# Attention over edges: a node block's sums kept and rescaled in four PSUM banks, and copied out at every step by ScalarE or VectorE

## The reference, cut to what matters

```python
q = (x @ Wq + bq).reshape(n, H, C)          # H = 8 heads, C = 32
k = (x @ Wk + bk).reshape(n, H, C)
v = (x @ Wv + bv).reshape(n, H, C)
alpha = einsum('ehc,ehc->eh', q[dst], k[src]) / sqrt(C)
amax = segment_max(alpha, dst)
ex = exp(alpha - amax[dst])
denom = segment_sum(ex, dst)
msg = (v[src] * (ex / denom[dst])[:, :, None]).reshape(-1, H * C)
out = segment_sum(msg, dst) + x @ Ws + bs
```

## Time and profile before

| | |
|---|---|
| median of the runs | 3828.62 us (3827.41, 3828.62, 3846.94) |
| the profiled execution, device time | 3797.8 us |
| its span | 3796.1 us |
| granted PE clock, mean over the span | 0.788 |
| DVE busy over the span | 2055.0 us (54%) |
| ACT busy over the span | 1393.1 us (37%) |
| PE busy over the span | 2511.5 us (66%) |

### The profile page before, as it was taken

The page is one execution under the profiler, slowest core; times in us unless marked ns, Lnnn a source line. Parts: engine busy times, 40 slices in busy tenths (PEclk is TensorE's granted clock), DMA queues, the critical chain, the costliest instruction groups (busy, mean ns, idle before and its releaser), DMA issues. The chain is left out here.

```text
span 3796.1 us, 40804 instructions
## 1 busy us (share of the span) xinstructions
PE 2511.5 (66%) x11176; PEld 1584.5 (42%) x11176; DVE 2055.0 (54%) x4110; ACT 1393.1 (37%) x3768; POOL 1735.3 (46%) x1762
## 2 busy tenths in 40 slices
PE   1894566666656325577987767777778666776872
PEld 0453444444444224424552422222227545665762
DVE  3443777777778926310007268888884511221388
ACT  0222444444443113331114468787882111111230
POOL 1344555555543052325665277777732255455100
PEclk9996777787878655578997868888889678888886
DMA  4003555555551000024312133333311211111104
GB/s 102 28 34 117 154 154 154 160 165 156 166 144 51 3 1 1 1 89 127 101 49 72 53 92 88 89 89 91 90 47 14 56 18 23 28 23 23 31 1 145
DMA packets 175765, 287.78 MB, mean 76 GB/s; under 512 B 56648, under 2 KB 118349, under 8 KB 175550
## 3 DMA queue, kind: packets, MB, share of 16 engines
q0 software_dynamic: 79568, 187.15, 18.3%
q1 hardware_dynamic: 80580, 75.89, 6.8%
q10 hardware_dynamic: 15402, 22.14, 1.7%
HBM read 248.79 MB, written 36.25 MB: 75 GB/s over the span
## 5 line engine op out<-in xcount | busy, mean ns | idle before, releaser
L911 POOL DMA_INDIRECT at_kv<-kv_tab,e_src x440 | 460.5, 1047 | 400.0 <-PE at_a L1043 272.0
L2270 PE MATMUL cv_ps<-cv_msg,cv_hot 128*128 128x512 f32 x880 | 508.7, 715 | 171.2 <-remote 61.4
L2257 POOL DMA_INDIRECT cv_x<-x_tab,e_src x440 | 470.4, 1069 | 239.6 <-issue 109.1
L2680 POOL DMA_INDIRECT gs_h<-h_tab,fc_q x312 | 297.8, 955 | 324.3 <-DVE gate_edge_rows L2764 151.5
L1957 POOL DMA_INDIRECT pairs<-gating_pair,gating_place x288 | 279.7, 971 | 345.2 <-SPq L1322 90.1
L2283 ACT ACTIVATE cv_msg<-cv_x,factors 128x64 f32<-128x64 f32 x1320 | 373.5, 335 | 95.4 <-issue 95.2
L2270 PEld LDWEIGHTS cv_ps<-cv_msg,cv_hot 128*128 128x128 f32 x880 | 174.6, 219 | 505.0 <-issue 204.6
L2320 DVE TENSOR_TENSOR acc<-acc,cv_ps 128x256 f32 x880 | 310.0, 416 | 121.4 <-issue 64.7
L1021 PE MATMUL at_q<-q_parts,at_hot_n 128*128 x1320 | 228.9, 328 | 85.9 <-DVE at_kv L1100 45.0
L2627 PE MATMUL gs_x_y<-x_w,gs_x_hid 128*128 128x256 f32 x640 | 194.8, 462 | 132.9 <-issue 119.4
L2650 DVE TENSOR_TENSOR gs_y<-gs_x_y,x_b 128x256 f32<-128x256 f32 x80 | 34.0, 425 | 441.0 <-DMA re_y<-expert_out,slot_i 239.6
(11 more groups left out here) (535 smaller groups left out, 4753.3 us busy)
## 6 DMA issues: line engine op xcount, KB each, us to landing
x_w<-in_L_ffn_w SPq DMA_DIRECT2D x16, 1024.0 KB
at_rel_row<-e_rel_rows SPq DMA_DIRECT2D x110, 128.0 KB
experts_out<-gs_y ACTq DMA_DIRECT2D x20, 512.0 KB, 2.6
x_y<-experts_out SPq DMA_DIRECT2D x20, 512.0 KB, 4.8
at_kv<-kv_tab,e_src POOLq DMA_INDIRECT x440
cv_x<-x_tab,e_src POOLq DMA_INDIRECT x440
kv_tab<-p_qkv SPq DMA_DIRECT2D x25, 256.0 KB, 2.0
gs_h<-h_tab,fc_q POOLq DMA_INDIRECT x312
```

Source lines behind the costliest of these rows:

```text
L911: nc.gpsimd.indirect_dma_start(out=kv[:, t % (RING * Q4), 0:2 * D], out_offset=None, in_=kv_tab, in_offset=bass.IndirectOffsetOnAxis(ap=e. ...
L2257: nc.gpsimd.indirect_dma_start(out=xg[:, i % RT, u, :], out_offset=None, in_=x_tab, in_offset=bass.IndirectOffsetOnAxis(ap=e.src[:, t:t + ...
L2270: nc.tensor.matmul(ps[u][:, :], hot[:, i % 2, u, :], msg[:, i % 2, u, :], start=True, stop=True).then_inc(summed, 1)
L2680: nc.gpsimd.indirect_dma_start(out=hg[:, i % RT, u, :], out_offset=None, in_=h_tab, in_offset=bass.IndirectOffsetOnAxis(ap=e.src[:, i * U ...
```

## The change

The two PSUM buffers of two banks become one of four banks. A block b keeps its sums in bank `b & 3` for as long as its steps last: matmuls of all its steps accumulate there, over batches too, and `rescale` multiplies the bank and not `acc`. Before every step a matmul of one column with the zero matrix opens the next block's bank (`bank(b + 1)`), so a block's first sum replaces what was there. There are no adds: at every step t, the bank of the block before (`b - 1`) is copied, 264 columns, to its place in `acc`, which is now shifted by one block, whether the block changed or not. ACT makes the copies of steps 0 to 7 of a batch, DVE those of steps 8 to 15. Copy t waits for all sums up to step t-1 and for copy t-1; PE opens a bank in step t only after copy t-2, and starts a batch only after `rescale`. ACT's order changes, with eight copies between its one-hots, and DVE's adds go, with copies later in the turn. The ring of rows that `node_hot` reads has three places and not four, the zero fill of `acc` is 264 columns and not 6,864, and PE opens all four banks once before its first `fetch`.

```diff
-    NHOT, NEDGE, NROW = 4, 3, 4
+    NHOT, NEDGE, NROW, R = 4, 3, 3, 4
-        ps_a = [s.ps(f"at_a{h}", [P, 2, 512]) for h in range(2)]
+        ps_a = s.ps("at_a", [P, R, 512])
+        def bank(b):
+            return ds(nc.s_assert_within(b & (R - 1), 0, R - 1, skip_runtime_bounds_check_because="two bits"), 1)
+        def copy_done(engine, t):
+            if t >= 0:
+                engine.wait_ge(copied[t % B16 // U], t // B16 * U + t % U + 1)
...
+                def copy(j, *steps):
+                    for x in steps:
+                        t = B16 * j + x
...
+                        if x == 0:
+                            here[j] = blocks_of(nc, mybir.EngineType.Activation, e, 2 * j)
+                        act.wait_ge(opened, 1)
+                        if t:
+                            act.wait_ge(summed, t)
+                            copy_done(act, t - 1)
+                        a(flat(acc[:, ds(here[j][x], 1), :]), flat(ps_a[:, bank(here[j][x] + (R - 1)), 0:W]),
+                          ACT.Copy).then_inc(copied[0], 1)
...
                     edge_hot(4 * j + 1)
+                    copy(j, 0, 1, 2)
+                    edge_hot(4 * j + 2)
+                    copy(j, 3, 4)
                     node_hot(4 * j + 8)
-                    edge_hot(4 * j + 2)
+                    copy(j, 5, 6, 7)
+                    edge_hot(4 * j + 3)
                     node_hot(4 * j + 9)
-                    edge_hot(4 * j + 3)
+                    edge_hot(4 * j + 4)
                     node_hot(4 * j + 10)
-                    edge_hot(4 * j + 4)
                     node_hot(4 * j + 11)
...
-                        if p >= 2:
-                            pe.wait_ge(added, p - 1)
-                        nc.tensor.matmul(ps_a[p % 2][:, 1, 0:W], nothing[:, 0:P], nothing[:, :], start=True, stop=False, skip_group_check=True)
-                        pe.wait_ge(built, p // 2 + 1)
-                        pe.wait_ge(weighted, p // 2 + 1)
+                        if x == 0 and j >= 1:
+                            pe.wait_ge(rescaled, j)
                         for u in range(2):
                             t = 2 * p + u
...
+                            b = where[p // Q4][Q4 * u + p % Q4]
+                            copy_done(pe, t - 2)
+                            nc.tensor.matmul(flat(ps_a[:, bank(b + 1), 0:1]), nothing[:, 0:P], nothing[:, 0:1],
+                                             start=True, stop=False, skip_group_check=True)
                             if u == 0:
...
+                                pe.wait_ge(built, p // 2 + 1)
+                                pe.wait_ge(weighted, p // 2 + 1)
+                            nc.tensor.matmul(flat(ps_a[:, bank(b), 0:W]), hot_e[:, t // Q4 % NEDGE, t % Q4, :],
+                                             kv[:, t % (RING * Q4), D:2 * D + H1], start=False, stop=False, skip_group_check=True).then_inc(summed, 1)
...
+                        dve.wait_ge(summed, t)
+                        copy_done(dve, t - 1)
+                        v.tensor_copy(flat(acc[:, ds(here[j][x - U], 1), :]), flat(ps_a[:, bank(here[j][x - U] + (R - 1)), 0:W])).then_inc(copied[1], 1)
...
-                    add(i, 0)
                     reduce(S, 1)
-                    add(i, 1)
                     weight(A, 2)
-                    load(2 * i + 1)
-                    add(i, 2)
                     multiply(at + 4)
-                    add(i, 3)
                     multiply(at + 5)
                     weight(A, 3)
-                    add(i, 4)
+                    copy(i, 8, 9)
                     reduce(S, 2)
-                    add(i, 5)
+                    copy(i, 10, 11)
                     multiply(at + 6)
+                    copy(i, 12)
                     multiply(at + 7)
+                    copy(i, 13)
...
-                    add(i, 6)
-                    add(i, 7)
+                    copy(i, 14, 15)
```

More of the change, by code:

```diff
@@ L867, in attention @@
         hot_e = s.sb("at_hot_e", [P, NEDGE, Q4, P])
-        nothing = s.sb("at_nothing", [P, W], BF)
+        nothing = s.sb("at_nothing", [P, P], BF)
         first_hot = s.sb("at_first_hot", [P, 2])
@@ L896, in attention, with flat @@
                 "crossed", "linked", "spread", "maxed", "fell", "faded", "squared", "spanned", "rescaled", "returned", "diffed", "exped",
-                "weighted", "summed", "added"))
+                "weighted", "summed", "opened"))
+        copied = [s.sem(f"at_copied{h}") for h in range(2)]
         def slot(hh):
             return slice(hh % RING * Q4, hh % RING * Q4 + Q4)
+        def bank(b):
+            return ds(nc.s_assert_within(b & (R - 1), 0, R - 1, skip_runtime_bounds_check_because="two bits"), 1)
+        def flat(ap):
+            return ap.rearrange("p a w -> p (a w)")
+        def copy_done(engine, t):
+            if t >= 0:
+                engine.wait_ge(copied[t % B16 // U], t // B16 * U + t % U + 1)
         def halves_of(j):
@@ L1045, in attend @@
                         if p % Q4 == Q4 - 1:
                             del where[p // Q4]
+                pe.wait_ge(cleared, 4)
+                for r in range(R):
+                    for o in range(0, W, P):
+                        ins = nc.tensor.matmul(ps_a[:, r, o:min(o + P, W)], nothing[:, 0:P], nothing[:, 0:min(P, W - o)],
+                                               start=(o == 0), stop=False, skip_group_check=True)
+                ins.then_inc(opened, 1)
                 for x in range(4):
@@ L1084, in _ @@
                 c = Chain(dve, chain)
-                base = {}
+                base, here = {}, {}
                 def load(i):
@@ L1117, in weight, with copy @@
                                     ALU.mult).then_inc(weighted, 1)
[L1119 to L1127, removed]
+                def copy(j, *steps):
+                    for x in steps:
+                        t = B16 * j + x
+                        if j < 0 or t >= T1:
+                            continue
+                        if x == U:
+                            here[j] = blocks_of(nc, mybir.EngineType.DVE, e, 2 * j + 1)
+                        dve.wait_ge(summed, t)
+                        copy_done(dve, t - 1)
+                        v.tensor_copy(flat(acc[:, ds(here[j][x - U], 1), :]), flat(ps_a[:, bank(here[j][x - U] + (R - 1)), 0:W])).then_inc(copied[1], 1)
                 def rescale(j):
```

30 lines of the change are left out of this document (13 added, 17 removed).

## The result

The changed kernel takes 3942.65 us (3937.04 to 3946.8, 4 runs), the kernel before on the same chip 3837.78 us (3827.41 to 3865.62, 4 runs): ratio 1.0261, interval 1.02 to 1.0321. That is +105 us where +33 was forecast, outside the range that ended at 3904. The profiled execution took 3946.8 us.

The account below looks back on a forecast made before the run. It took DVE's own order of work, some 23 us of a 29.3 us batch, plus PE's late answers, as the bound. 15 x 1.1 + 12 x 1.5 - 3, with 0.1 for registers, made +33: 3862 us, range 3804 to 3904.

Parts of the forecast that it names:

- waits for ACT's copies: Likeliest rival: in attention, one-hots between ACT's copies make PE and DVE wait; +33 us, chance 0.42.
- DVE's own gain: DVE's work in a batch: adds go, copies come, 1.6 us gained from work alone.
- ACT gains eight copies, and they set the pace of PE: ACT's copies 0 to 7 stand between one-hots; copy 2 ends at 755.9, copy 7 at 762.0 us.
- So DVE waits: DVE at copies 8 and 9: new waits of 2.3 and 0.3 us, so the batch loses 1.0 us at `scored`.
- 1.1 and 1.5: Loss in us a batch: 1.1 at the full clock, 1.5 in some 12 batches with sums at the low clock.
- The tail gives nothing back: Batch's end: PE's step and fetches keep the scan no earlier than 1.7 us after the hole's addition.
- PE's steps get longer: PE's openings and weight load: 0.1 us more a step at full clock, twice that at 1.2 GHz; duo 1.2 us.
- The register work: Register work in the pairs of copies: another 0.1, taking the sum from +31.5 to +33 us.
- At nothing: Terms put at no cost: `rescale` in PSUM, PE's wait for it, three row places, register loads.
- At the start: Stage's start: the 5.78 us fill goes, giving 3 us, of between 0 and 5.
- PE as the bound: Rival: PE itself becomes the bound, its weight load showing in full; +65 us, chance 0.18.
- the faster case: Rival: copies 0 to 7 are done when DVE comes to copy 8; -54 us to 3775, chance 0.18.

Follow-up runs that it names:

- e7: Changed kernel with every second attention gather left out, on the chip where the kernel before takes 3243.92 us: 3310.35 us, ratio 1.0208.
- e8: Kernel before with every second attention gather left out, on the chip where the kernel before takes 3243.92 us: 3245.53 us, ratio 1.001.
- e5: Changed kernel with bank numbers worked out in registers ahead of the waits on PE, ACT and DVE: 3290.66 us, ratio 1.0152.
- e18: Changed kernel with registers hoisted, four one-hot steps ahead of ACT's exponentials and every second attention gather left out: 3676.91 us, ratio 0.9572.
- e17: Kernel before with every second attention gather left out, on a chip with standstills: 3657.07 us, ratio 0.952.
- e9: Changed kernel as it is, run again on a chip with standstills: 3910.63 us, ratio 1.0259.
- e10: Kernel before as it is, run again on a chip with standstills: 3805.6 us, ratio 0.9992.
- e15: Changed kernel with two edge_hot steps ahead of ACT's exponentials and registers worked out ahead of the waits, second run: 3932.78 us, ratio 1.0222.
- e14: Changed kernel with hoisted registers and two edge_hot steps, first and node_hot all ahead of ACT's exponentials: 3920.14 us, ratio 1.0196.
- e12: Changed kernel with two edge_hot steps ahead of ACT's exponentials and registers worked out ahead of the waits, first run: 3891.38 us, ratio 1.0204.
- e1: Changed kernel with PSUM banks taken by the step's number instead of the block's, output not the attention's: 3837.45 us, ratio 1.0042.
- e2: Changed kernel without the one-column opening matmul of each step, output not the attention's: 3885.47 us, ratio 1.0164.
- e4: Kernel before with 11 unread semaphore increments of PE ahead of each fetch: 3955.91 us, ratio 1.0338.
- e6: Changed kernel with banks by step number and no opening matmuls, output not the attention's: 3236.26 us, ratio 0.997.

## Why the prediction was wrong, step by step

The direction and the mechanism of the likeliest rival, waits for ACT's copies, were right. The size was not: the step that failed is the wait at copy 8, put at 2.3 us and measured at 3.5. And one large thing was missing.

*DVE's own gain, 1.6 us a batch:* right, 1.9 measured (e7 against e8).

*"ACT gains eight copies, and they set the pace of PE":* right, and exact from copy 2 to copy 7: 6.1 us foretold, 704.42 to 710.50 is 6.1. DVE comes to copy 8 at 8.1 us after the first `weight` (699.23 to 707.30), foretold 8.0.

*"So DVE waits", 2.3 us:* the term that was mis-sized. It is 3.6 in the changed kernel's batch and 3.8 in that of e7, 3.5 on the mean of 25 batches in each. The mistake is the start: I took the sums of steps 0 and 1 from one batch of before, so that copy 2 ended 4.1 us after the first `weight`. It ends 5.2 after it in the batch shown (704.42), 5.0 on the mean. Of these 1.1 us some 0.8 are the batch that I read: there DVE had waited 0.99 us for the spread factors (L1136) just ahead of the first `weight`, PE was that much further in its `fetch`, and the first sum starts 1.36 us after the `weight` (751.80 to 753.16). That is the least of 25 batches of that trace; their mean is 2.3. In the changed kernel it starts 2.15 us after (699.23 to 701.38), 2.1 on the mean. Some 0.2 us more are the two steps at half clock, and 0.1 is ACT's. The row of before, then the two of now:

```profile
750.94 0.23 DVE L1136 TENSOR_SCALAR at_shrink<-at_t,at_first_hot 128x8 f32<-128x8 f32 x1 [0.99 <-PE at_t L1079]
```

```profile
701.38 1.23 PE L1071 MATMUL at_a<-at_kv,at_hot_e 128*128 128x264 f32 x2
...
702.48 1.23 PE L1071 MATMUL at_a<-at_kv,at_hot_e 128*128 128x264 f32 x2
```

I had added the longer steps at the tail of a batch and not here, where ACT's order carries them on. With 0.47 instead of 0.3 at copy 9 and chained pairs of 0.82 instead of 0.6, `scored` comes 2.8 us later, not 1.0. Whoever puts these in place of 1.1 and 1.5 gets the own cost of the change: 2.7 us (27.53 less 24.87) to 3.3 (28.15 less 24.84) a batch, 72 to 89 us over 27.

*The tail gives nothing back:* right, 1.60 us against 1.7 foretold.

*PE's steps get longer, a duo of 1.2 us:* 1.12, with 0.11 to 0.12 a step for the opening and the load where 0.16 was taken. The row's 207 ns, or the two thirds that I took of it, was too much; no row tells which.

*The register work:* no run shows the 0.1 that the sum has for it in the pairs. What they show: in the changed kernel's trace 317 of the 432 register instructions of DVE's copies (its sequencer's ALU_OP records) run while DVE is idle, behind the wait, and 115 beside its work; hoisted (e5) all 432 run beside it. Hoisting them left 1.0152 [1.0122, 1.0182] (e5) where e7 has 1.0208 [1.0176, 1.024]; e7 has half of the gathers, which cost nothing there (e8). So it is about 0.5 points, 18 us.

*At nothing:* right for the register loads and for `rescale`. In the attention stage of before 45 of DVE's 55 register loads run wholly beside its work, the one at 757.62 us for 0.34 us among them, and in the changed kernel 53 of 54. `rescale` takes 0.17 and 0.43 us, in SBUF (751.33, 751.46) as in PSUM (698.76, 698.89).

*At the start, -3 us:* 0. The fill of 5.78 us had hidden in the wait for the first gathers.

*The other rivals:* PE as the bound did not come about: the clock granted in the stage fell from 0.78 to 0.76 only, and PE's longer steps can be no more than what is left with the repaired order, 0.8 us a batch (e18, 25.67, less e17, 24.84); the faster case needed ACT at copy 7 by the time DVE is at copy 8, and e18 shows that even then (0.58 us of wait) the kernel is not below e17.

*What was missing:* the standstill. I had seen waits without a releaser and booked them as PE's lateness, unchanged by the edit. (The batch was 30.7 us, too, and not 29.3, since 821 us hold fewer than 28; so 7 to 8 us of it, not 6, were not DVE's own work.) Standstills and stretches cost the kernel before 4.8 points (e17 against the whole: 0.952) and the changed one 4.9 to 5.3 (0.973 against 1.0222 to 1.0261). So in the difference of 105 us they are a small part: with half of the gathers the two kernels lie 2.1 points apart, some 80 us; without stretches at all, 2.0 (e7 less e8). By these what they add is between nothing and 25 us, within the uncertainty; by the batches it is 1.2 us a batch (4.5 between e9 and e10, on one chip, less 3.3), some 33 us. But they change what a repair is worth: 1.6 points without them, 0.1 to 0.5 with them (e15, e14 and e12 against the changed kernel, each on one chip).

What stays open: why stretches are elastic, so that time won ahead of one is lost in it, and why fixed banks pay under them (2.0 points) where early and hoisted work does not. e1 differs from e12 in how many instructions there are, and not only in where they stand: the traces record 38750 of PE, DVE and ACT in e1, 39738 in e2, 41937 in the changed kernel, 37871 before, and the ratios 1.0042, 1.0164, 1.022 to 1.026, 1 follow that order, though not in proportion. e4 does not fit in: it has 40236 and the highest ratio, 1.0338. Fixed banks were not run without stretches other than with the openings gone too (e6, 0.997), so how much of their gain is the chain's is not known. What the gathers' traffic holds up, the semaphores' way or another, no run here shows. One rival is left untested: that the profiler's recording has a part in it. The chips with standstills have records of fewer semaphore updates, 20712 in the changed kernel's trace against 42722 in that of e5, and every run here has a recorded span and clock; whether the engines stand still without recording is not known.

No version beats the kernel before on the reference's result; e6, which does by 0.3 points, leaves out what makes the banks right.

## What to carry to other kernels

When copies or other small steps are put on an engine with idle time, lay them out in that engine's own order: idle time ahead of the batch is worth nothing to a copy that stands behind 3.3 us of other work. A chain over three engines starts with the first sum, so read where that starts in many batches: the one batch that I read had it 1 us earlier than the mean. Address arithmetic written after a wait runs after the wait (317 of 432 register instructions here, 0.1 to 0.16 us a chained copy): compute it ahead. And waits without a releaser that come at the same place in a train of DMAs are a thing of its own: take part of the traffic away before any sum is built on them, since under them a repair can show little.

## What was not expected of the hardware

On chips where the kernel before takes 3,799 to 3,856 us PE and DVE stand nearly still once a batch, and in the kernel before ACT too, for up to 8 us, while the gathers go on. In the changed kernel PE's register instructions take 0.7 us there instead of 0.046. On one chip, where the kernel before takes 3,244 us, nothing of the kind shows. Leaving out half of the attention's gathers takes 4.8 points off the kernel before on the first kind of chip and nothing on the second (1.001). The granted clock of the whole execution was 0.788 in the profile of before and 0.845 in that of e8.
